# Attention scores of a graph layer: two edge tiles share a PSUM tensor and are combined by one operation each

## The reference, cut to what matters

```python
h = (x @ W.T).reshape(n, H, D)                      # n = 3125 nodes, H = 8 heads, D = 32
src, dst = (edge_index[0], edge_index[1])           # 50000 edges, sorted by dst
alpha = jnp.einsum('ehd,hd->eh', h[src], a_src) + jnp.einsum('ehd,hd->eh', h[dst], a_dst)
enc = jax.nn.relu(edge_attr @ edge_W.T + edge_b).reshape(-1, H, D)
alpha = alpha + jnp.sum(enc * h[dst], axis=-1)
alpha = jnp.where(alpha >= 0, alpha, 0.2 * alpha)   # then a softmax over the edges of a node
```

## Time and profile before

| | us |
|---|---|
| three runs, median (lowest to highest) | 9028.0 (9024.55 to 9036.87) |
| the profiled execution | 9012.47 |
| its span, first to last instruction | 9010.7 |
| PE, DVE, ACT, POOL busy | 4843.6, 2995.5, 1822.5, 4642.9 |
| the stage changed, first gather to the next stage's first operation | 5654.73 to 6296.11 = 641.4 |
| the same stretch of `edge_sums` | 7453.25 to 7987.92 = 534.7 |

### The profile page before, as it was taken

The page is one execution under the profiler, slowest core; times in us unless marked ns, Lnnn a source line. Parts: engine busy times, 40 slices in busy tenths (PEclk is TensorE's granted clock), DMA queues, the critical chain, the costliest instruction groups (busy, mean ns, idle before and its releaser), DMA issues. The chain is left out here.

```text
span 9010.7 us, 79716 instructions
## 1 busy us (share of the span) xinstructions
PE 4843.6 (54%) x17334; PEld 3383.6 (38%) x17335; DVE 2995.5 (33%) x8688; ACT 1822.5 (20%) x4291; POOL 4642.9 (52%) x4486
## 2 busy tenths in 40 slices
PE   0020464464380676477556374888368984527464
PEld 0010342343250565123334263344246764415353
DVE  6850002002205564100100203677572133337601
ACT  0000342332110001143334121232103331110021
POOL 0777677676675775477477574565000006730022
PEclk9999776677595777799877587798788995559687
DMA  1201332332231442177233263555240006735154
GB/s 41 56 3 11 103 105 51 96 105 58 56 84 55 135 137 76 37 210 210 75 105 105 58 198 100 170 179 157 98 145 14 10 14 194 211 88 182 66 174 136
DMA packets 496397, 926.06 MB, mean 103 GB/s; under 512 B 125846, under 2 KB 322012, under 8 KB 493047
## 3 DMA queue, kind: packets, MB, share of 16 engines
q0 software_dynamic: 224000, 477.10, 20.4%
q1 hardware_dynamic: 272119, 445.72, 14.6%
HBM read 727.74 MB, written 193.59 MB: 102 GB/s over the span
## 5 line engine op out<-in xcount | busy, mean ns | idle before, releaser
L773 PE MATMUL ps<-bufb 128*125 128x257 f32 (+2 forms) x3328 | 1341.7, 564 | 1413.0 <-ACT bufb L667 713.4
L640 POOL DMA_INDIRECT bufa<-tablea,list_dst x832 | 795.2, 956 | 1561.1 <-DVEq L2328 1116.4
L640 POOL DMA_INDIRECT bufb<-table,list_dst x1248 | 1266.4, 1015 | 548.3 <-issue 362.8
L773 PEld LDWEIGHTS ps<-bufb 128*125 128x125 f32 x3328 | 789.0, 249 | 1965.2 <-issue 1839.4
L640 POOL DMA_INDIRECT bufb<-table,list_src x832 | 786.8, 946 | 319.0 <-issue 244.9
L243 POOL DMA_INDIRECT edges_src<-bufb,slots x400 | 504.0, 1260 | 362.7 <-ACTq L337 220.8
L243 POOL DMA_INDIRECT edges_dst<-list_dst,slots x400 | 545.0, 1363 | 217.6 <-issue 132.8
L2631 PE MATMUL ps<-list_src,bufa 128*125 128x264 f32 x1664 | 441.0, 422 | 326.5 <-DVE bufa L674 236.2
L291 POOL DMA_INDIRECT edges_sorted<-list_dst,slots x416 | 398.8, 959 | 305.6 <-issue 130.3
L2631 PEld LDWEIGHTS ps<-list_src,bufa 128*125 128x125 f32 x1664 | 332.0, 205 | 435.1 <-issue 371.6
L1382 POOL DMA_INDIRECT tokens<-bufb,small x125 | 148.6, 1189 | 605.2 <-PEq L1377 561.5
(11 more groups left out here) (454 smaller groups left out, 8518.5 us busy)
## 6 DMA issues: line engine op xcount, KB each, us to landing
passed<-bufa SPq DMA_DIRECT2D x208, 512.0 KB, 3.7
bufa<-passed SPq DMA_DIRECT2D x208, 512.0 KB, 4.3
bufb<-in_L_ffn_W SPq DMA_DIRECT2D x128, 512.0 KB
bufa<-lows SPq DMA_DIRECT2D x52, 512.0 KB, 4.1
bufb<-table,list_dst POOLq DMA_INDIRECT x1248, 3.3
bufb<-in_L_ffn_W SPq DMA_DIRECT2D x16, 1024.0 KB, 8.4
bufb<-tokens SPq DMA_DIRECT2D x64, 256.0 KB, 2.7
answers<-bufb SPq DMA_DIRECT2D x64, 256.0 KB
```

The source lines that it names most:

```text
L640: pool.indirect_dma_start(out=rows(t % RT), out_offset=None, in_=table, in_offset=bass.IndirectOffsetOnAxis(ap=lst[:, t, 0:1].bitcast(I32) ...
L773: pe.matmul(ps[:B, ds(banks.at[j], W)], onehot[:, j, :], rows[:, j, :], start=False, stop=False, skip_group_check=True).then_inc(summed, 1)
```

## The change

- The two spreads of a pair of tiles go into the two banks of one PSUM tensor `pw[i]` of 2 x 512 floats; there are two of these. PE holds once for each pair, until DVE has combined the pair before the last, and only the second matmul of a pair counts `spread_done`.
- DVE takes a pair up with one product of 2 x 256 and one sum of 2 x 8, in place of two of each. The sum no longer has the mask.
- To make room for four banks of `pw`, the transposed records `pr` lie in the unused upper half of the banks of `pt`.
- At the end, when all groups are scored, one DVE operation over the 416 x 8 scores of each partition adds 0.2 times the mask (before, the mask went through the leaky ReLU, which for a large negative number is the same).

```diff
-        pr, pw, pe_ = ([psum(f"{n}{i}") for i in range(2)] for n in ("pr", "pw", "pe"))
+        pe_ = [psum(f"pe{i}") for i in range(2)]
+        pw = [nc.alloc_psum_tensor(m.name(f"pw{i}"), [P, 2, 512], F32) for i in range(2)]
         pt = [nc.alloc_psum_tensor(m.name(f"pt{i}"), [P, 1024], BF16) for i in range(2)]
+        pr = [pt[i][:, EG * P:].bitcast(F32) for i in range(2)]
@@ combine (DVE)
-                    for j in range(g * EG, (g + 1) * EG):
+                    for j in range(g * EG, (g + 1) * EG, 2):
                         q = j % (2 * EG)
-                        tgt = pw[j % 2]
-                        v.wait_ge(spread_done, i * RT + (j + 1))
-                        if j % 2 == 0:
-                            v.wait_ge(enc_done, i * (RT // 2) + (j // 2 + 3))
-                        v.tensor_tensor(enc[:, q, :], enc[:, q, :], tgt[:, 0:D], ALU.mult)
-
-                        v.scalar_tensor_tensor(sums[:, j, :], rows[:, j, D:W], lst[:, ds(i * RT + j, 1), 6],
-                                               tgt[:, D:W], ALU.add, ALU.add).then_inc(combined, 1)
-                    v.wait_ge(combined, i * RT + (g * EG + EG + 2))
+                        tgt = pw[j // 2 % 2]
+                        v.wait_ge(spread_done, i * (RT // 2) + (j // 2 + 1))
+                        v.wait_ge(enc_done, i * (RT // 2) + (j // 2 + 3))
+                        v.tensor_tensor(enc[:, q:q + 2, :], enc[:, q:q + 2, :], tgt[:, :, 0:D], ALU.mult)
+                        v.tensor_tensor(sums[:, j:j + 2, :], rows[:, j:j + 2, D:W], tgt[:, :, D:W],
+                                        ALU.add).then_inc(combined, 1)
+                    v.wait_ge(combined, i * (RT // 2) + (g * 2 + 4))
@@ after the last group (DVE)
                 write_groups(v, (one_hots, 3), (combine, 0))
+                a3 = alpha.rearrange("p (t h) -> p t h", h=H)
+                v.wait_ge(scored, RING + GROUPS)
+                v.scalar_tensor_tensor(a3, lst[:, :, 6:7].broadcast_to([P, NT, H]), 0.2, a3, ALU.mult, ALU.add)
@@ spreads (PE)
                     for j in range(g * EG, (g + 1) * EG):
-                        hold(pe, combined, i * RT + (j + 1))
-                        pe.matmul(pw[j % 2][:, 0:W], onehotT[:, j, :], HB[:, ds(blocks[j % EG] * W, W)], start=True,
-                                  stop=True).then_inc(spread_done, 1)
+                        if j % 2 == 0:
+                            hold(pe, combined, i * (RT // 2) + (j // 2 + 1))
+                        mm = pe.matmul(pw[j // 2 % 2][:, j % 2, 0:W], onehotT[:, j, :],
+                                       HB[:, ds(blocks[j % EG] * W, W)], start=True, stop=True)
+                        if j % 2:
+                            mm.then_inc(spread_done, 1)
```

## The result

| | before | changed |
|---|---|---|
| median of four runs each (lowest to highest), us | 9031.1 (9024.6 to 9036.9) | 8929.8 (8912.9 to 8934.8) |
| profiled execution, span | 9012.5, 9010.7 | 8930.2, 8928.4 |
| changed stage, first gather to the next stage's first operation | 641.4 | 6209.83 - 5671.66 = 538.2 |
| its gathers, first to last | 624.3 | 6191.96 - 5671.66 = 520.3 |
| mean granted clock, share of the stage at the low level | 0.86, 29% | 0.91, 18% |

The ratio is 0.9885 (95% interval 0.9868 to 0.9902), 101 us less; forecast were 83 and a range of 8922 to 9000. The stage alone gave 103.2. The two profiled spans differ by only 82.3.

A forecast was written before the change was run, and what follows sets the result against it. PE and DVE were taken to bound the stage, gathers next. The larger bound, 552 us, plus 5 gave 557, saving 84; less 1.5 for the mask, 82.5, so 9028.0 - 83 = 8945 us, range 8922 to 9000.

The forecast's parts named there:

- The bound and the next bound: Changed stage: PE and DVE bound it by waiting for each other; POOL's gathers come next, 98 us away.
- DVE's step: DVE's combination of spreads: product of two tiles 0.69 us, sum near 0.22, saving 0.4 us a group.
- PE's group: PE's time for one group in the changed stage: 4.5 us at the full clock, 8.2 at the low.
- The stage, 557: Changed stage without the mask: PE's bound 552 us, POOL's 545, plus 5 for taking turns: 557, saving 84.
- the first groups: Start of the changed stage: first four groups at 8.2 us, POOL having room for four, add 8 us to POOL's bound.
- The clock: PE's clock in the changed stage: share of time at the low level kept at 28%, mean clock 0.80 to 0.95.
- The rule weighed in the prediction: PE's clock: the skill page puts falls down to long gaps between matmul bursts; the prediction said the trace doesn't agree.
- The mask: DVE's single mask operation at the stage's end: costs 1.5 us, between zero and 7.2.
- Coupling that stays: Changed stage: engines still wait in a ring, groups 5.0 to 5.1 us at full clock; 8980 to 9005 us; chance 0.20.
- A colder clock, slower than before: Changed stage: PE idling in each gather-bound group lowers its clock; at 65% low share 9068 us; chance 0.07.
- A clock that stays high: Changed stage: clock high after the first 41 us, POOL the bound; 8933 us; chance 0.08.
- Spreads that aren't uncoupled: Changed stage: holds or PSUM stop PE as before; within 10 us of no change, 9018 to 9032; chance 0.05.

The follow-up runs named there:

- the repeat: The changed kernel, unchanged, timed once more against the kernel before: ratio 0.989, median 8934.8 us, changed stage 540.4 us.
- the run with one pair: Against the kernel before, DVE's merged operations with only one two-bank PSUM tensor for the spreads: ratio 1.0401, stage 1013.8 us; on the slower chip 1.0253, 1015.4 us.

## Why the prediction was right, and where its terms were off

- **The number.** The medians fell by 101 us, where 83 were forecast. That the profiled executions differ by 82.3 us, almost the 82.5 forecast, is chance: the stage gave 103.2, and stages that the change doesn't touch took 20.9 of it back in this pair.
- **The bound and the next bound.** Right. PE and DVE waited for each other, and the gathers were next: POOL's waits fell under the 50 us named, and the stage came within 4 us (within 6 in the repeat) of the 534.7 of `edge_sums`.
- **Which wait carries it.** Right in the mechanism, and too generous to DVE. The prediction gives both parts as if both were needed; the run with four one-bank tensors shows that the spreads' room alone does it, and the run with one pair that the merge alone loses. DVE's step was measured as forecast: 684 ns for the product and 163 for the sum against 690 and 220.
- **PE's group.** Forecast 4.5 us at the full clock between 4.3 and 4.79, measured 4.23: both the hold and the wait for the block numbers went, so it lies a little below the lower bound. At the low clock 8.17 against 8.2.
- **The stage, 557.** This term was mis-sized, by some 20 us: without the mask, as it was meant, the stage took 536.5. It took PE's 536 + 16 and POOL's 534.7 + 8 + 2.4 as bounds that lie side by side, and added 5 us for taking turns. With 4.23 in place of 4.5 PE has 0.77 us a group in hand, so a low stretch of 14 us is won back in some 7 groups. Of the 8 us for the first groups 0.2 came, as the clock rose after 15 us and not 41. In the repeat it rose after 25 us, and 1.6 came. The kernel before had 25 us in its repeat too, so part of this is the luck of the execution; what a low start of 41 us costs the changed kernel wasn't seen. The end took 13.2 us from the last gather to the last score, against 10.3 in `edge_sums`: 2.8, where 2.4 was put.
- **The clock.** I kept the low share of 28%, and it fell to 18% (15% in the repeat). It isn't what made the stage shorter: with half the encodings the low share was 32% and the stage just as long. The rule weighed in the prediction, from the Trainium skill (TensorE: Matmul & The Clock Gate, section "HAM oscillation — how this bites in real kernels"), would have kept the clock up where PE has no long gap. By it the run with twice the encodings, PE busy 832.69 of 839.30 us, would stay at 1.00; it was at 0.73. The measurement decides against it here, as far as a modelled busy time can tell. Another section of that page of the Trainium skill, "A second HAM failure mode: psum-queue depth-cycling", has the clock oscillate where PE idles briefly between groups of matmuls for the sake of PSUM. The run with one pair, with its 1.11 us hold in each group, agrees that such holds go with a low clock, but there it didn't oscillate; it stood at 0.50.
- **The mask.** Forecast 1.5 us between 0 and 7.2, measured 2.57. The guess that the stores would hide most of it failed: in `edge_sums` the next stage followed 4.45 us after the last score, here, without the mask, 2.14. That the stores set the 4.45 isn't in the row, which names PE's sequencer at the barrier.
- **The rivals.** Coupling that stays: its mark, POOL waiting some 80 us, is absent. A colder clock, slower than before: not in this change. A stage at 0.50 throughout did come with one pair, at 9.64 us a group rather than 8.2, and not with the idle time of a stage bound by its gathers, as the rival had it, but with a hold amid the spreads. A clock that stays high: its time, 8933, was the nearest of all to the 8930 measured, though the clock did fall 15 times; the falls were short enough to be hidden. Spreads that aren't uncoupled: PE's waits for DVE before spreads, 37.6 us before, are gone.
- **The sum.** With the mask the stage was forecast at 558.5 us and measured at 538.2. Of the 20.3 between them 11.9 are what PE's bound and the turns were put above the gathers' bound (557 - 545.1), 7.8 the first groups, 1.2 the end behind the last score (4.71 in place of 4.45 + 1.5), and 0.6 went the other way, in the gathers' pace and the work behind the last gather.

## What to carry to other kernels

Where two engines pass tiles through a ring, try room first and merging second: two more buffers took PE's wait of 0.45 us and DVE's of 0.53 out of a group, while merging without room made PE's wait 1.11 us, and the clock stayed low with it. Estimate the gain from a stage that is already bound by the next resource; it was within 4 to 6 us here, closer than the sum over the engines (some 20 us off). And put a step that can go either at the end or beside the bound engine's work beside it, even if it becomes a hundred small operations.

## What was not expected of the hardware

- PE's clock fell to 0.50 with PE busy 10.20 of 10.20 us, and was at that level for 53% of a stage in which PE was busy 832.69 of 839.30 us.
- With a hold of 1.11 us amid the spreads of each group the clock stayed at 0.50 for a stage of 1012 us, on both chips; without the hold it rose after 11 to 25 us in each run of the changed kernel and its other variants on the first kind.
- One chip ran the kernel before in 9962 us and another in 9031. On the slower one DVE and ACT stood still for up to 8.3 us about every 20 us in the changed stage, and there were stops in untouched stages too; a change of 1.1% on one was one of 0.5% on the other.
- The last gathered rows of a stage land late. In the changed kernel a group's rows were there 2.9 us (median of 104 groups) after the issue of its last gather, but those of the last three groups after 6.6, 8.2 and 10.2 us; the product that needs the last waited 3.84 us for them.
